# Criss-cross attention: the value projection with 128 positions stationary and 512 weight columns streaming, and the bias added on GpSimd

## What is computed

```python
q = einsum('oc,bchw->bohw', Wq, x) + bq        # 64 channels
k = einsum('oc,bchw->bohw', Wk, x) + bk
v = einsum('oc,bchw->bohw', Wv, x) + bv        # 512 channels
energy_H = einsum('bchw,bcgw->bhwg', q, k) - 1e30 * eye(H)
energy_W = einsum('bchw,bchv->bhwv', q, k)
att = softmax(concat([energy_H, energy_W], -1), -1)
out = gamma * (sum_g v * att_H + sum_v v * att_W) + x
```

## Time and profile before

| | us |
|---|---|
| median of three runs | 3737.39 |
| the profiled execution, first to last instruction | 3739.5 |
| TensorE busy | 3683.0 (98%) |
| VectorE busy | 2674.2 (72%) |
| ScalarE busy | 1533.3 (41%) |
| GpSimd busy | 649.6 (17%) |
| DMA, mean rate | 233 GB/s |

### The profile page before, as it was taken

How to read it: one execution, slowest core, us unless ns; L and a number is a source line. 1 busy time by engine, 2 the same in 40 slices (tenths; PEclk the granted TensorE clock), 3 DMA queues, 4 the chain that set the end, 5 groups by cost and what they waited for, 6 DMA issues and landing times.

```text
span 3739.5 us, 67129 instructions
## 1 busy us (share of the span) xinstructions
PE 3683.0 (98%) x26968; PEld 3663.5 (98%) x26968; DVE 2674.2 (72%) x4324; ACT 1533.3 (41%) x2130; POOL 649.6 (17%) x816
## 2 busy tenths in 40 slices
PE   8799999999999999999999999999999999999999
PEld 7799999999999999999999999999999999999999
DVE  8767787677876778767786677866778657786555
ACT  7523444244442445424454244542444424444111
POOL 1410023100331003210042000420004200042000
PEclk9899999999999999999999999999999999999999
DMA  8687768877698776977769777697776977769665
GB/s 268 178 230 254 254 215 234 245 253 248 203 246 247 240 256 191 259 237 254 247 190 255 242 245 254 196 251 240 259 232 204 250 229 255 230 210 254 204 211 180
DMA packets 333956, 873.97 MB, mean 234 GB/s; under 512 B 34640, under 2 KB 186704, under 8 KB 333648
## 3 DMA queue, kind: packets, MB, share of 16 engines
q1 hardware_dynamic: 333648, 869.67, 75.9%
HBM read 661.92 MB, written 207.62 MB: 233 GB/s over the span
## 4 chain that ended last, share of the span: by engine, by line
PE 96%; DVE 3%; DMA 1%; issue 0%; ACT 0%; SPq 0%; POOL 0%; DVEq 0%; POOLq 0%
PE bank L1044 43%; PE bank L1011 19%; PE bank L1032 18%; PE bank L960 10%; PE bank L972 3%; PE bank L981 3%; DVE E L735 1%; PE bank L996 0%; DVE Sx L714 0%; DVE Sx_first L714 0%; DMA XT_r<-in_x_row 0%; DVE mx_c L730 0%; DVE mx_r L730 0%; DVE zs_c L745 0%; DMA XA_first<-in_x 0%
## 5 line engine op out<-in xcount | busy, mean ns | idle before, releaser
L1044 PE MATMUL bank<-Sy,Wv_hi 128*128 128x384 f32 x6144 | 1595.3, 340 | 8.6 <-DVE Sy L719 8.6
L1044 PEld LDWEIGHTS bank<-Sy,Wv_hi 128*128 128x128 f32 x6144 | 1089.0, 189 | 9.8 <-DVE Y L809 9.8
L1044 PE MATMUL bank<-Sy,Wv_lo 128*128 128x384 f32 x3072 | 1028.5, 335 | 0.0
L809 DVE SCALAR_TENSOR_TENSOR Y<-bank,bv_sb,Y 128x384 f32<-128x384 f32 x768 | 470.3, 612 | 723.9 <-PE bank L1044 723.1
L1032 PE MATMUL bank<-Pt,XT_r 128*128 128x96 f32 x6144 | 719.3, 275 | 3.7 <-DMA XT_r<-in_x_row 3.7
L1032 PEld LDWEIGHTS bank<-Pt,XT_r 128*128 128x128 f32 x6144 | 715.9, 192 | 4.4 <-DMA XT_r<-in_x_row 4.1
L484 POOL TENSOR_TENSOR Pe<-Pe,F 128x384 f32<-128x384 f32 x336 | 286.0, 853 | 2389.5 <-DMA Pe<-e_scratch 2351.0
L617 ACT ACTIVATE Sy<-Y 128x768 fp32r<-128x768 f32 x384 | 319.0, 842 | 793.4 <-PE bank L1044 747.3
L1044 PEld LDWEIGHTS bank<-Sy,Wv_lo 128*128 128x128 f32 x3072 | 577.4, 188 | 0.0
L605 ACT ACTIVATE Y<-bank 128x384 f32<-128x384 f32 x384 | 326.9, 851 | 429.3 <-PE bank L1011 429.3
L793 DVE COPY Y<-bank 128x384 f32<-128x384 f32 x384 | 317.7, 827 | 214.5 <-PE bank L1011 198.0
(11 more groups left out here) (73 smaller groups left out, 3030.2 us busy)
## 6 DMA issues: line engine op xcount, KB each, us to landing
XT_r<-in_x_row SPq DMA_DIRECT2D x384, 384.0 KB, 6.0
Y<-in_x SPq DMA_DIRECT2D x192, 768.0 KB, 5.5
out<-Y SPq DMA_DIRECT2D x184, 768.0 KB, 4.2
XA<-in_x SPq DMA_DIRECT2D x180, 768.0 KB, 6.4
XT_r<-in_x_col SPq DMA_DIRECT2D x192, 384.0 KB, 8.2
XT_c<-in_x_col SPq DMA_DIRECT2D x192, 384.0 KB, 8.0
e_scratch<-E SPq DMA_DIRECT2D x384, 144.0 KB, 3.0
Pe<-e_scratch SPq DMA_DIRECT2D x336, 144.0 KB, 7.6
```

The costliest lines, as they stand in the source:

```text
L809: nc.vector.scalar_tensor_tensor(at, proj_ps[c % 2][:, 0:CP], bv_sb[:, c:c + 1], at, op0=ALU.add, op1=ALU.add).then_inc(out_made, 1)
L1044: last = nc.tensor.matmul(proj_ps[c % 2][:, 0:CP], w[:, ct, at], Sy[:, lo, ct, :], start=(ct == 0 and k == 0), stop=(ct == CT - 1 and k == 2))
```

## The change

The projection swaps its operands. Before, a 128 x 128 block of Wv was stationary and 384 positions streamed. Now 128 positions of the sums are stationary and all 512 output channels stream, so that a chunk is three tiles of 12 matmuls. The result has positions on the partitions, hence residual and output lie that way (`x_pos`, `out`, moved by the same number of DMAs of the same size, except that the last chunk of a batch is stored in three parts for four). The bias can no longer be a scalar of a partition: it becomes a full tile `gbv`, and GpSimd adds it to the loaded residual, 1536 elements a partition, once a chunk (`add_bias`). `finish` becomes an addition of two tensors, 512 wide, three a chunk. `round_y` and `low_y` work on three tiles of 4 x 128 elements for two halves of 768. The order of the iterations on TensorE, ScalarE and VectorE is written anew, and `add_bias(n + 1)` stands behind `scale(n + 4)` on GpSimd.

```diff
-            def project(b, n, c):
-                pe.wait_ge(out_made, past(out_made, (b * CHUNKS + n) * CT + c - 1))
-                at = slice(c * P, (c + 1) * P)
+            def project(b, n, t):
+                k = tile_no(b, n, t)
+                pe.wait_ge(out_made, past(out_made, k - 2))
+                pe.wait_ge(y_lo_made, past(y_lo_made, k))
+                at = slice(t * P, (t + 1) * P)
                 for ct in range(CT):
...
+                    for lo, w in ((0, Wv_hi), (0, Wv_lo), (1, Wv_hi)):
+                        last = nc.tensor.matmul(proj_ps[k % 2][:, :], Sy[:, lo, ct, at], w[:, ct, :],
+                                                start=(ct == 0 and lo == 0 and w is Wv_hi), stop=(ct == CT - 1 and lo == 1))
...
+            def add_bias(b, n):
+                j = n % 2
+                pool.wait_ge(xres_in[j], past(xres_in[j], 16 * (b * (CHUNKS // 2) + n // 2 + 1)))
+                at = Y[:, out_slot(n), :, :].rearrange("p c n -> p (c n)").rearrange("p (t c) -> p t c", t=TILES)
+                nc.gpsimd.tensor_tensor(at, at, gbv[:, :].unsqueeze(1).to_broadcast((P, TILES, C)), ALU.add)\
+                    .then_inc(bias_added, 1)
...
-                nc.vector.scalar_tensor_tensor(at, proj_ps[c % 2][:, 0:CP], bv_sb[:, c:c + 1], at,
-                                               op0=ALU.add, op1=ALU.add).then_inc(out_made, 1)
+            def finish(b, n, t):
+                k = tile_no(b, n, t)
+                dve.wait_ge(proj_summed, past(proj_summed, k))
+                if t == 0:
+                    dve.wait_ge(bias_added, past(bias_added, b * CHUNKS + n + 1))
+                nc.vector.tensor_tensor(out_tile(n, t), proj_ps[k % 2][:, :], out_tile(n, t), ALU.add)\
+                    .then_inc(out_made, 1)
...
+            def low_y(b, n, t):
+                dve.wait_ge(y_hi_made, past(y_hi_made, tile_no(b, n, t)))
+                nc.vector.tensor_tensor(tile_of(Sy[:, 1, :, :], t), tile_of(Y[:, n + 1, :, :], t),
+                                        tile_of(Sy[:, 0, :, :], t).bitcast(F32), ALU.subtract).then_inc(y_lo_made, 1)
```

More of the change, by code:

```diff
@@ L844, in row_stage @@
                     finish(b, n, 0)
-                    if more and n + 1 == A_FIRST:
-                        low_x(b + 1, 0)
+                    after, attended = n + 1 < CHUNKS, n + 2 < CHUNKS
+                    if after:
+                        low_y(b, n + 1, 0)
                     if b_now and b_now[0]:
                         sum_z(b + 1, CHUNKS + b_now[0] - 1)
-                    if a_now:
-                        low_x(b + 1, a_now[1])
-                        shift(b + 1, a_now[0])
                     if b_now:
@@ L889, in row_stage @@
                         sum_z(b + 1, CHUNKS + b_now[2])
-                    if n + 2 < CHUNKS:
+                    if after:
+                        low_y(b, n + 1, 2)
+                    if attended:
                         add_row(b, n + 2, 2)
```

194 lines of the change are left out of this document (101 added, 93 removed).

## The result

The changed kernel takes 3865.85 us (median of four runs, 3862.12 to 3871.65), beside 3737.79 us for the kernel before on the same chip: a ratio of 1.0347, 95% interval 1.0335 to 1.036. It is slower by 128 us. The forecast was 3820 with a range to 3865, so the direction was right, and the time lies 0.85 us over the range.

A forecast was written before the change was run, and what follows sets the result against it. TensorE, busy 98% of 3739.5 us, was taken as the bound. 3739.5 - 31 (matmuls) - 9 (iteration 23) + 87 (a) + 14 (b) + 22 (end) = 3822.5, given as 3820 for the runs' median; range 3705 to 3865.

The forecast's parts named there:

- Matmuls, -31: Projection: 36 matmuls of 512 columns for 48 of 384, at 0.2267 us each, save 0.16 us a chunk, 192 chunks.
- no gain at 512 columns: Rival on the projection: time goes all with columns, 0.2311 us a matmul; 3851 us with the waits; chance within the forecast's 0.57.
- The shorter matmuls: Rival on the projection: 0.2133 us a matmul, 123 us less in all; 3728 with waits (chance 0.05), 3620 without (0.03).
- Waits of iteration 23, -9: Head of iteration 23: eight TensorE waits of about 1.1 us, 8.6 in all, go because `low_y` works tile by tile.
- ScalarE at nothing: VectorE's and ScalarE's own work in the new kernel: nothing on the path, so no cost in the sum.
- The bias's length, 3.3 us: GpSimd's `add_bias` of 1536 elements: four times `scale`'s 0.83 us at most, taken as 3.3 us.
- The a iterations, +87: 84 a iterations: the bias gets between the halves of `low_x`; TensorE waits 1.3 us in 0.8 of them.
- The b iterations, +14: 35 b iterations: `gather_k` behind the bias makes TensorE wait 1.3, 0.6 and 0.1 us, 2 us a batch, seven batches.
- The end, +22: End of the row stage: the last `mask` stands behind a bias, so TensorE waits 3.1 us for the factors, seven times.
- misses low_x: Rival in the a iterations: loads land so that the bias does not meet `low_x`; 3736 us, no change; chance 0.12.
- costs nothing: Rival: GpSimd's long instruction holds nothing up, as VectorE slips in or slack swallows it; 3710 us; chance 0.16.
- Half of it: Rival: a wait in every second a iteration; 3770 us; chance 0.07.

The follow-up runs named there:

- e1_no_bias: The changed kernel without GpSimd's bias addition (bias left out of the output; `finish` waits for the residual's load itself): 3741.53 us, ratio 1.0013.
- e9_orders_no_bias: e1_no_bias with `gather_q` of groups 0 and 1 ahead of `round_y` in iteration 18, and a batch's last `low_y` behind the column factors: 3720.95 us.
- e12_late_both: Changed kernel, bias in spread thirds, the last chunk's added in the next column stage, plus both orders of e9_orders_no_bias: 3735.02 us, ratio 0.9991.

## Why the prediction was right or wrong

Here is the difference of the two traces by stage, cut at the first projection matmul of the chunks. (14.6 us of `project_kq`, which stood ahead of that cut before and behind it now, are counted with the a iterations in both.) e1_no_bias splits each into swap and bias.

| us | forecast | measured | of it the swap | the bias |
|---|---|---|---|---|
| plain iterations | -10 | -9.0 | -9.2 | +0.2 |
| a iterations | +74 | +64.1 | -0.6 | +64.7 |
| b iterations | -1 | +26.6 | +1.8 | +24.8 |
| iteration 23 and column stage | +21 | +39.1 | +6.2 | +32.9 |
| program | +83 | +121.0 | -2.0 | +123.0 |

The forecast's swap was -29 (matmuls -31, waits -9, factors +11), its bias +112. So of the 38 us that were missed, 27 are the swap and 11 the bias. The step that failed is not the main one, the meeting with `low_x`, but what stood around it: the gain of the matmuls was taken at its best end, ScalarE's new order and the clock behind a stall were put at nothing, and the waits of the b iterations and of the end were too short.

- **Matmuls, -31: mis-sized.** I took the end at which 13 ns of each instruction are fixed. The pitch is 0.2297 in the mean, nearer to 0.2311, nothing gained, than to 0.2267. The plain iteration lost 0.06 us for 0.16, the a iteration 0.01; about 8 us in all. The rival of no gain at 512 columns was the better choice, and the argument "something is likely fixed" held sharply in one place of the order and was worth little in the others. The shorter matmuls (0.213) are refuted. The formula that the Trainium skill gives for the gap of isolated matmuls ("TensorE: Matmul & The Clock Gate", section "Back-to-back issue gap") comes to 215.8 ns, an estimate from that page; the trace disagrees, with 224 at the least.
- **Waits of iteration 23, -9: right.** All 8.6 us are gone. Iteration 22, at whose end they stood, is 12.54 us long before and 11.25 in e1_no_bias; 0.99 of that is the wait, the rest the matmuls.
- **ScalarE at nothing: wrong by 12.8 us.** "The rewritten order ... is costed at nothing" was said of TensorE; of ScalarE the prediction says "Nothing on the path" from the lengths of instructions alone, and its new order was not gone through. In iteration 18 `gather_q` stands behind `round_y`, which waits for a whole tile. e9_orders_no_bias is the proof: moved ahead, the wait is gone.
- **The bias's length, 3.3 us: near.** 3.50 by its median.
- **The a iterations, +87: mechanism right, too many hits.** The start (7.58 us for 7.3), the turn between the halves, and the price of a hit (18.73 - 17.47 = 1.26 us for 1.3) were as worked out. But 51 of 84 iterations were hit, six in ten and not eight: where the bias starts at 6.5 to 8.0 it meets `low_x`, in the other 33 at 8.1 or later. I had read the loads' landing times of the trace before as if they were the same here: in its a iterations 19 of 84 loads took over 6.1 us, in the kernel after 31. 51 x 1.26 = 64. This term is too large by 23 us, and it was luck that it covered a part of what the others lacked.
- **The b iterations, +14: too low by 11.** Iterations 19 to 22 are 0.3, 1.5, 0.8 and 0.9 us longer than without a bias, 3.5 us a batch for the 2.0 that were worked out. The kind of wait was right (`gather_k` behind the bias, 1.3, 0.9 and 0.26 us idle in batch 0), but `low_y` and `gather_k` hold each other in turn, and I had summed them once.
- **The end, +22: a wait of the right kind, for another reason and too short.** In six batches the last `mask` was not held up; `low_y` met the bias of the last chunk head-on (4.11 us), and everything behind it came 3.4 us later. A wait of 4.5 us for the forecast's 3.1 is some 9 us, and the clock that fell after it, at nothing in the sum, 10 more.

Of the rivals, "misses low_x" (3736) and "costs nothing" (3710) are refuted by the 51 hits. "Half of it" asked for 42 hits and the forecast for 67, so in the a iterations that rival was the nearer one; its 3770, though, halves the other waits too (42 hits at 1.3 us alone would give 3788). The nearest of all is "no gain at 512 columns", 3851. The range failed by adding up: five terms short by about 23, 13, 11, 9 and 10 us against one too large by 23 (43 in sum for the 38 missed, as each was measured by itself), while its upper end allowed for the a iterations at their worst or for no gain of the matmuls, and not for several at once.

Of the signs that the prediction named, `low_x` over 3 us in half of the a iterations or more came (51 of 84), and so did the length and the start of `add_bias` (3.50 and 7.58 us) and the end of the waits at iteration 23. The waits for `low_x` stayed under its 60 us: 56.6 in all, 45.3 of them in the a iterations. `gather_k` cost 15.3 us idle for 14, the factors 30.2 for 22, and the pitch was 0.2297 for 0.227.

## What to carry to other kernels

Work that is put on an idle GpSimd is paid by VectorE's instructions with two SBUF inputs, for the length of one GpSimd instruction at a time: hold that length (not the engine's busy share) against the slack of each such instruction nearby, cut it into parts shorter than that slack, and put the parts where VectorE reads PSUM or nobody waits (in the kernel after, 248 `finish` ran beside a GpSimd instruction and none took over 0.69 us). Here the same 192 additions cost 123 us in one piece and 14 us or less spread out (e12_late_both over e9_orders_no_bias). When an order is rewritten, go through every engine's list. And for each stall of TensorE, see whether the sum contains what the clock does after it.
